# Two openings and the step between convolution and scan of a one-core vision kernel, put in another order

## What is computed

```
h = fno(x)                              # fc0, 4 x (rfft2, mix 20x20 modes, irfft2, pointwise, gelu), fc1, fc2
h = concat(cls_tok, h)                  # 128 x 65 tokens of 64 channels
h = h + attn(layernorm(h));  h = h + ffn(layernorm(h))

# inside attn, over windows of 32 tokens:
xm, z = split(x @ inproj_w.T);  xm = silu(causal_conv(xm, conv_w) + conv_b)
dt, B, C = split(xm @ xproj_w.T, [16, 32])            # 16, 16 and 16 columns
delta = softplus(dt @ dtproj_w.T + dtproj_b);  A = -exp(A_log)
h_t = exp(delta_t * A) * h_(t-1) + (delta_t * xm_t) * B_t
y_t = sum_n(h_t * C_t);  y = (y + xm * Dp) * silu(z);  out = y @ outproj_w.T
```

## Time and profile before

| | us |
|---|---|
| three runs | 6218.33, 6227.20, 6225.49 |
| their median | 6225.49 |
| the profiled execution, its own time | 6217.95 |
| its span | 6215.1 |
| first product of PE in the first program | 60.42 |
| last clearing barrier between the programs, first memset of POOL | 4846.69 |
| first turn of maps in the second program | 4894.87 |
| second block: first `draw` product, and its first sum of softplus | 5237.11, 5257.57 |

### The profile page before, as it was taken

One profiled execution on the slowest core, in us unless ns is written; L12 is line 12 of the kernel. 1 busy time (PEld: TensorE's weight loads), 2 busy tenths in 40 slices (PEclk: granted clock), 3 DMA queues, 4 the chain that ended last, 5 costly groups with the idle time before them and its releaser, 6 DMA issues. The chain is left out here.

```text
span 6215.1 us, 273887 instructions
## 1 busy us (share of the span) xinstructions
PE 5483.1 (88%) x119165; PEld 4105.8 (66%) x119165; DVE 2829.8 (46%) x4392; ACT 2677.2 (43%) x4990; POOL 1103.7 (18%) x1049
## 2 busy tenths in 40 slices
PE   5999999999999989989989999999999588888888
PEld 4877787677868876778677767876786243434343
DVE  2444344344434443444344434443443374848483
ACT  2334433443353335333533353344334364647473
POOL 3221222032203221222222122212220000000000
PEclk9999999999999999999999999999999798989898
DMA  2111111111111110111011101111110100000000
GB/s 33 15 14 15 20 14 14 15 19 14 14 17 18 14 22 12 15 21 18 10 20 19 14 14 21 14 15 17 14 14 4 22 1 8 1 8 1 4 1 4
DMA packets 443120, 85.55 MB, mean 14 GB/s; under 512 B 437624, under 2 KB 437896, under 8 KB 441832
## 3 DMA queue, kind: packets, MB, share of 16 engines
q1 hardware_dynamic: 441960, 67.78, 8.7%
HBM read 63.52 MB, written 4.23 MB: 11 GB/s over the span
## 5 line engine op out<-in xcount | busy, mean ns | idle before, releaser
L217 POOL COPY x_T<-x_X 128x512 f32<-128x512 f32 x1024 | 1074.5, 1105 | 3586.0 <-ACTq L791 3418.4
L786 ACT ACTIVATE x_X<-ga 128x512 f32<-128x512 f32 x1280 | 751.8, 598 | 1083.3 <-PE ga L458 899.2
L642 DVE COPY x_X<-ev 128x512 f32<-128x512 f32 x640 | 438.7, 689 | 842.5 <-PE ev L477 793.0
L458 PEld LDWEIGHTS ga<-pw_rhs,x_X 64*64 64x64 f32 x32768 | 595.0, 135 | 279.5 <-issue 278.2
L642 DVE COPY V<-ev 104x512 f32<-104x512 f32 x608 | 411.5, 690 | 599.3 <-PE ev L424 440.4
L489 PEld LDWEIGHTS ev<-dft_consts,x_T 128*64 128x64 f32 x16384 | 577.1, 137 | 42.0 <-issue 41.8
L489 PE MATMUL ev<-dft_consts,x_T 128*64 128x80 f32 x16384 | 598.1, 233 | 4.9 <-POOL x_T L217 3.4
L458 PE MATMUL ga<-pw_rhs,x_X 64*64 64x64 f32 x32768 | 587.0, 218 | 4.8 <-issue 4.1
L450 PE MATMUL ga<-V,inv_w 40*64 40x512 f32 x4096 | 550.0, 604 | 28.9 <-ACT V L754 27.9
L642 DVE COPY Y<-ev 128x400 f32<-128x400 f32 (+1 forms) x768 | 463.3, 603 | 208.5 <-PE ev L489 164.4
L642 DVE COPY D<-ev 128x512 f32<-128x512 f32 x576 | 362.3, 685 | 337.8 <-PE ev L396 335.5
(11 more groups left out here) (213 smaller groups left out, 8216.4 us busy)
## 6 DMA issues: line engine op xcount, KB each, us to landing
mix_w<-in_sw SPq DMA_DIRECT2D x128, 400.0 KB, 8.0
coords<-in_coords SPq DMA_DIRECT2D x66, 96.0 KB, 2.1
maps<-Y SPq DMA_DIRECT2D x128, 16.0 KB
raw<-maps SPq DMA_DIRECT2D x8, 256.0 KB, 3.6
out<-out_t SPq DMA_DIRECT2D x8, 256.0 KB, 3.5
w<-in_w SPq DMA_DIRECT2D x3, 512.0 KB, 6.6
fc_rhs<-in_fc_w SPq DMA_DIRECT2D x32, 0.4 KB
dft_consts<-in_dft SPq DMA_DIRECT2D x1, 336.0 KB
```

Source lines behind the costliest of these rows:

```text
L217: pool.tensor_copy(x_T[:, :, H * bc + h0:H * bc + h0 + 16].rearrange("p c (s n) -> p c s n", n=2), blocks.rearrange("p (s a n c) -> p a c ...
L458: last = pe.matmul(ps[HALF * bp:HALF * bp + HALF, HALF * s:HALF * s + HALF], x_X[r:r + HALF, g, col:col + HALF], pw_rhs[r:r + HALF, :], st ...
L642: dve.tensor_copy(dst, src).then_inc(ev_taken, 1)
L786: x_new = act.activation(blocks.rearrange("p (s a n) -> p s a n", s=8, a=2)[:, :, bc, :], ga[n % N_GA][:, :].rearrange("p (s n) -> p s n", ...
```

## The change

In `fno_program` the opening is ordered by need. POOL sets `fc0_rhs` and `coords` first, then S and `mix_w`; DVE clears the other six tiles itself. SP issues group 0's coordinates, the lower half of `fc0_rhs`, group 1's coordinates, and then the other small loads, which PE now waits for only ahead of the first mixing. ACT issues the Fourier constants, the bias columns and the upper half of `fc0_rhs` on its own queue (22 DMAs). The unused coordinates at the end are loaded ahead of the last maps' stores.

In `token_program` POOL clears the padded tiles first; ACT issues 18 `early` DMAs, SP the raw maps of block 0 and then the rest. `sel` and the bf16 identity are made by POOL, with no memset of `sel`. PE waits for the `later` weights only ahead of the product with `inproj`, and no longer for A (though it still waits for `out_ready`, which DVE signals behind A's sign change).

Between convolution and scan, B and C are made by one product of 32 columns, and `xc` is gone. DVE copies B, and splits C on token rows (128 partitions, 256 columns, into `gate_p`, which the experts use later); eight bf16 products turn the parts to where the spread reads them, and DVE copies them to `parts`. ACT loads the Exp table behind Silu by a one-column Exp, takes abs and exp by pieces, and ln by pieces; DVE adds by pieces as they come.

```
+        zeroed_pool = [S[:, :, :, :, :].rearrange("p a g b k -> p (a g b k)"),
+                       mix_w[:, :, :].rearrange("p a b -> p (a b)")]
+        zeroed_dve = [inv_h[:, :], pw_all[:, :, :].rearrange("p a b -> p (a b)"),
+                      fc2_lhs[:, :, :].rearrange("p a b -> p (a b)"), dc_bias[:, :, :].rearrange("p a b -> p (a b)"),
+                      D[:, :, :].rearrange("p a b -> p (a b)"), V[:, :, :].rearrange("p a b -> p (a b)")]
...
+            pool.memset(fc0_rhs[:, :], 0.0).then_inc(cleared, 1)
+            pool.memset(coords[:, :, :].rearrange("p a n -> p (a n)"), 1.0).then_inc(cleared, 1)
+            for tile in zeroed_pool:
                 pool.memset(tile, 0.0).then_inc(cleared, 1)
...
+        first_act = [(consts[:, :], t["dft"])]
+        for l in range(LAYERS):
+            first_act.append((cb_raw[:, l:l + 1], t["cb"][l].rearrange("(c a) -> c a", a=1)))
+        first_sp, once = [], []
+        for r, queue in ((0, first_sp), (HALF, first_act)):
+            for h in range(16):
+                queue.append((fc0_rhs[r + 3 * h:r + 3 * h + 3, CH * h:CH * h + CH], t["fc0_w"]))
+            queue.append((fc0_rhs[r + 48:r + 49, :].rearrange("p (h c) -> p h c", c=CH),
+                          t["fc0_b"].rearrange("(a x c) -> a x c", a=1, x=1).to_broadcast([1, 16, CH])))
+        N_FIRST = 16 * (len(first_sp) + len(first_act))
...
+            sp.wait_ge(cleared, 2)
             load_coords(0, 0)
-            load_coords(0, 1)
             with nc.allow_non_contiguous_dma(reason="small weights, once"):
+                for dst, src in first_sp:
+                    sp.dma_start(dst, src).then_inc(first_in, 16)
+                load_coords(0, 1)
+                sp.wait_ge(dve_cleared, len(zeroed_dve))
                 for dst, src in once:
-                    sp.dma_start(dst, src).then_inc(const_in, 16)
+                    sp.dma_start(dst, src).then_inc(mixw_in, 16)
+            sp.wait_ge(cleared, 2 + len(zeroed_pool))
             load_mix(0)
...
+                if last_coords is not None:
+                    last_coords()
...
+            pe.wait_ge(first_in, N_FIRST)
...
+                    pe.wait_ge(mixw_in, (chunk * LAYERS + to + 1) * (16 * J) + 16 * len(once))
...
+            pe.wait_ge(bias_ready, 1)
...
+            for tile in zeroed_dve:
+                last = dve.memset(tile, 0.0)
+                last.then_inc(dve_cleared, 1)
+            dve.wait_ge(dve_cleared, len(zeroed_dve))
+            dve.wait_ge(first_in, N_FIRST)
...
+            dve.wait_ge(cleared, 2 + len(zeroed_pool))
...
+            act.wait_ge(cleared, 2)
+            with nc.allow_non_contiguous_dma(reason="small weights, once"):
+                for dst, src in first_act:
+                    act.dma_start(dst, src).then_inc(first_in, 16)
...
-        xc = sb("xc", [DI, 2, 2 * DS])
-        padded.append(xc[:, :, :].rearrange("p h n -> p (h n)"))
-        for hf in range(2):
-            loads.append((xc[:, hf, DS * hf:DS * hf + DS], t["xproj"][:, DTR + DS:DTR + 2 * DS]))
...
+        first_tiles = {id(tile) for tile in (ident, center, average, cls, in_w, in_b, ln_g, ln_b, xproj, dtproj, A)}
+        early = [(tile, src) for tile, src, of in loads if id(of) in first_tiles]
+        later = [(tile, src) for tile, src, of in loads if id(of) not in first_tiles]
+        N_ZERO = 1 + len(decay)
...
+            for tile in padded:
+                pool.memset(tile, 0.0).then_inc(S_(padded_ready), 1)
             pool.memset(eps[:, :], EPS).then_inc(S_(zeroed), 1)
...
+            pool.wait_ge(S_(early_in), 16 * len(early))
+            pool.wait_ge(S_(zeroed), N_ZERO)
+            pool.tensor_copy(ident16[:, :], ident[:, :]).then_inc(S_(ident16_ready), 1)
+            pool.wait_ge(S_(ident16_ready), 1)
+            for q in range(3):
+                if q:
+                    pool.wait_ge(S_(sel_ready), q)
+                r = slice(32 * q, 32 * q + 32)
+                pool.tensor_copy(sel[r, :, :], ident[r, r].rearrange("p (n a) -> p n a", a=1).to_broadcast([32, 32, P]))\
+                    .then_inc(S_(sel_ready), 1)
...
-            sp.wait_ge(S_(zeroed), N_ZERO)
-            with nc.allow_non_contiguous_dma(reason="small weights, once"):
-                for dst, src in loads:
-                    sp.dma_start(dst[tuple(slice(None) for _ in dst.shape)], src).then_inc(S_(weights_in), 16)
-                sp.dma_start(gate_b[:, :], t["gate_b"].rearrange("(a e) -> a e", a=1).to_broadcast([P, NE]))\
-                    .then_inc(S_(weights_in), 16)
...
             load_raw(0)
+            sp.wait_ge(S_(padded_ready), len(padded))
+            with nc.allow_non_contiguous_dma(reason="small weights, once"):
+                for dst, src in later:
+                    sp.dma_start(dst[tuple(slice(None) for _ in dst.shape)], src).then_inc(S_(weights_in), 16)
+                sp.dma_start(gate_b[:, :], t["gate_b"].rearrange("(a e) -> a e", a=1).to_broadcast([P, NE]))\
+                    .then_inc(S_(weights_in), 16)
...
+            pe.wait_ge(S_(early_in), 16 * len(early))
+            pe.transpose(psB[0:DTR, 0:DI], xproj[:, 0:DTR], ident[:, :]).then_inc(S_(xdt_turned), 1)
             pe.wait_ge(S_(xdt_ready), 1)
-            pe.matmul(psA[:, BC:BC + DI], xdt_t[:, :], dtproj[:, :], start=True, stop=True).then_inc(S_(draw_w_made), 1)
-            pe.wait_ge(S_(consts_ready), 1)
+            pe.matmul(psB[:, BC:BC + DI], xdt_t[:, :], dtproj[:, :], start=True, stop=True).then_inc(S_(draw_w_made), 1)
...
+                pe.wait_ge(S_(weights_in), 16 * (len(later) + 1))
...
-                    for hf in range(2):
-                        at = HB * hf + c
-                        last = pe.matmul(psB[0:2 * DS, c:c + n], xc[:, hf, :], u[:, at:at + n],
-                                         start=hf == 0, stop=hf == 1)
-                last.then_inc(S_(xbc_ready), 1)
+                wait(sz_ready)
                 for j, (c, n) in enumerate(rows):
-                    last = pe.matmul(psB[0:n, HB + DS * j:HB + DS * j + DS], u[:, c:c + n], xproj[:, DTR:DTR + DS],
-                                     start=True, stop=True)
-                if win == 1:
-                    for j, (c, n) in enumerate(rows):
-                        last = pe.matmul(psB[0:n, HB + BC + DS * j:HB + BC + DS * j + DS], u[:, c:c + n],
-                                         xproj[:, DTR + DS:DTR + 2 * DS], start=True, stop=True)
+                    last = pe.matmul(psB[0:n, HB + 2 * DS * j:HB + 2 * DS * j + 2 * DS], u[:, c:c + n],
+                                     xproj[:, DTR:DTR + 2 * DS], start=True, stop=True)
                 last.then_inc(S_(b_turned), 1)
-                wait(pos_ready, len(cuts))
                 if win > 1:
-                    wait(parts_ready)
+                    pe.wait_ge(S_(ident16_ready), 1)
+                    wait(c_split)
+                    for j in range(nt):
+                        last = pe.matmul(psB[0:96, P * j:P * j + P], gate_p[:, j, :, :].rearrange("p s a -> p (s a)"),
+                                         ident16[:, :], start=True, stop=True)
+                    last.then_inc(S_(cT_ready), 1)
...
+                    wait(parts_ready)
...
+                pe.wait_ge(S_(sel_ready), 3)
...
+            act.wait_ge(S_(padded_ready), len(padded))
+            with nc.allow_non_contiguous_dma(reason="small weights, once"):
+                for dst, src in early:
+                    act.dma_start(dst[tuple(slice(None) for _ in dst.shape)], src).then_inc(S_(early_in), 16)
+            act.wait_ge(S_(early_in), 16 * len(early))
...
+                act.activation(std_first[:, :], eps[:, :], ACT.Exp)
                 for c, n in cuts:
                     wait(draw_ready)
 
                     act.activation(both(delta, w, c, n), paired(psA, c, n), ACT.Abs, bias=dt_b[:, :])\
                         .then_inc(S_(abs_ready), 1)
-                wait(b_turned)
+                    wait(abs_ready)
+                    act.activation(both(delta, w, c, n), both(delta, w, c, n), ACT.Exp, scale=-1.0)\
+                        .then_inc(S_(exp_ready), 1)
+                for c, n in cuts:
+                    wait(exp_ready)
+                    act.activation(both(delta, w, c, n), both(delta, w, c, n), ACT.Ln, bias=1.0).then_inc(S_(ln_ready), 1)
                 m = 2 * NT if w == BLK else 2
-                act.activation(b_t[0:tp, 0:m, :], psB[0:tp, HB:HB + DS * m].rearrange("p (j n) -> p j n", n=DS), ACT.Copy)\
-                    .then_inc(S_(b_copied), 1)
-                wait(abs_ready, len(cuts))
...
-            dve.wait_ge(S_(weights_in), 16 * (len(loads) + 1))
             dve.wait_ge(S_(zeroed), N_ZERO)
-            for q in range(3):
-                r = slice(32 * q, 32 * q + 32)
-                dve.tensor_copy(sel[r, :, :], ident[r, r].rearrange("p (n a) -> p n a", a=1).to_broadcast([32, 32, P]))
-            dve.tensor_copy(ident16[:, :], ident[:, :])
```

(33 more changed lines are left out.)

84 lines of the change are left out of this document (24 added, 60 removed).

## The result

| | before | after |
|---|---|---|
| runs, us | 6217.9 to 6227.2 (4 runs) | 6132.2 to 6140.61 (4 runs) |
| median, us | 6221.91 | 6139.37 |
| profiled execution, its span | 6217.95, 6215.1 | 6138.44, 6135.5 |

The ratio of the times is 0.9867, with a 95% interval of 0.9848 to 0.9887: faster by 1.3%. The forecast was 6132.8 with a range of 6110 to 6156. The time lies 6.6 us above the forecast and inside the range. Between the two profiled executions 79.6 us of span went, where my sum had 92.7. The table follows the same events through both traces; a row's gain is what is added to the lead on the way to that event.

What follows compares the result with a forecast made beforehand. Bound mostly by the untouched Fourier network (some 4775 of 6215 us); touched were idle openings and block chains. 45.7 + 4.0 + 32.6 - 11 + 19.2 + 2.2 = 92.7, from 6225.5 to 6132.8; range 6110 to 6156.

Steps and rivals of the forecast that it cites:

- rival (3): Both openings: two issue queues are no faster than one; time 6146, chance 0.08.
- PE waits 2 us: First opening: PE wants group 2's coordinates at 40.1, they land behind `mix_w` at 42, so it waits 2 us.
- the middle of two theories: Second opening: POOL's casts cost DVE between 0 and 22 us; the forecast took 11.
- rival (1): Second opening: POOL's casts hold DVE in full, 17 to 22 instead of 11; time 6139 to 6144, chance 0.20.
- 3c less 4.6: Second opening: three DVE operations wait c - 1.2, c - 2.4 and c - 1.0 for a cast of c.
- With the rise in the middle of them: Between convolution and scan: PE's clock rises during second `draw` or B and C; gain 4 to 5 a block, 4.8 taken.
- it never rises, gain 2: Between convolution and scan: PE's clock stays low, B and C end at 5253.3, gain 2 us a block.
- upper clock, 6.9: Between convolution and scan: PE at its upper clock, the sum starts at 5250.6, gain 6.9 us a block.
- (2): Second opening: POOL's casts cost DVE nothing; time 6122, chance 0.12.
- (4): Between convolution and scan: PE's clock is up in all four blocks, gain 28 instead of 19; time 6124, chance 0.08.
- (5): Scan: PE stays at its lower clock, a step costs up to 3.2 more; slower than before, 6261 with 40 steps, chance 0.03.
- (6): First opening: loads still end with the `once` list, 18 us of the gain go; time 6151, chance 0.04.

Runs made afterwards that it cites:

- the casts held back: The change with POOL's three casts of `sel` held back until block 0's input projection is there: 0.9858 of before, `inproj` 33.8 us behind the barrier (change 44.0).
- this part alone: The kernel before with only the change between convolution and scan: 0.9951 of before.
- the product in halves: The change with the product of B and C in halves, the first half's 16 matmuls between the two draws: 0.9867 of before.

## Why the prediction was right, and where its steps were not

- **First opening, 45.7 forecast, 39.8 measured at the projection of group 3.** The start was right: 13.42 instead of 12.7, ACT's list from 2.19 to 10.76 (forecast 2.3 to 10.3), and two queues as fast as hoped, so rival (3) fell. The failed step is "PE waits 2 us". The wait was named and its place was right, its size was not: `mix_w` took 10.75 us to issue, not 8.4, the coordinates were issued at 39.10, not at 36.9, and landed 6 us later. And the sum left out the clock: a wait of 4.1 us cost 7.2 to 7.4 with the lower clock behind it. The last 6.3 us up to the network's end are inside the scatter between executions, which no sum could have had.
- **End of the first program, 4.0 forecast, 5.1 measured.** The fc2 product is followed by the barrier within 6.8 us instead of 11.8. Right, a little small.
- **Second opening, 32.6 forecast, 32.3 measured.** The turn of the maps stands 15.9 behind the barrier (15.7 to 16). The early weights landed about 0.9 us later than forecast. What made that up is that A's sign change was not in the way: `out_ready` went out at 4824.0, when that operation began and not when it was over, so the step "PE still waits behind DVE's two copies, A's sign change and `out_ready`, 2.5 in all" was too long by 0.6: it took 1.9.
- **POOL's casts, 11 forecast, 9.6 measured, 10.2 against the casts held back.** The number was right by luck, as it was the middle of two theories. The mechanism was that of rival (1), with c = 3.63 instead of 7 to 8.8: the three operations took 7.9 us longer than usual (2.12 + 3.15 + 3.09 less 3 x 0.17), of which 5.75 reached PE. The prediction's own formula, 3c less 4.6, gives 6.3 with this c (and 16.4, not 17, at c = 7). The other 3.8 us are a term that neither theory had: PE, idle behind the operations, ran the variance and spread products at the lower clock. The mis-sized term is the cast. It was costed at the rate of POOL's copy of 512 columns, and went 2.4 times as fast. The rule of the Trainium skill, SBUF — State Buffer, section "Who interferes with whom", that the second of the two waits for the whole instruction of the other, agrees with the ends of the three operations, which fall on the ends of the casts within 0.03 us. As a mechanism it was better than the middle; with the cast priced at 8.8 it would have given 22, further off than the 11.
- **Between convolution and scan, 19.2 forecast, 13.3 measured** (22.0 in the trace of this part alone). The pieces are as forecast: second `draw` at +5.3, 3.78 or 2.0 long, ACT ready at 13.7 (forecast 13.5), the product 3.65 to 4.1 or 6.87 (3.75 or 7.3). Two steps failed. "With the rise in the middle of them" assumed that PE's clock would rise during the second `draw` or the product, as it had in the kernel before; it stays down through a product of 6.87 us in about half of the blocks, and in the product in halves it stays at 0.50 for the last 10.2 of 12.7 busy us. So the case "it never rises, gain 2" (2.0 to 2.7 measured) and the case "upper clock, 6.9" (5.9) both occur, about evenly. And I did not see that DVE waits in the wrong order, though the price of the product stood in the text: putting the sums first makes the stretch 17.1 to 17.5 at either clock.
- **Tail, 2.2 forecast, 2.3 measured.** The first sum starts 3.7 us behind `draw` instead of 6.2, and DVE's idle time in front of it fell from 2.78 to 1.09 us.
- **Other rivals.** (2) fell with the 9.6 us, (4) with three of four blocks at the lower clock, (5) since from `draw` to the gate turn a block at the lower clock takes 187.4 us and at the upper one 184.1, and 3.1 of these 3.3 are the step itself (21.5 and 18.35), so there is no slower scan behind it; from the turns of `du` on, a block took no longer than before. (6) fell with the first product at 13.42.
- **The sum.** 92.7 less 5.2 (stall) less 6.3 (network) less 5.9 (blocks), plus 2.7 elsewhere in the blocks and 1.6 in the small terms, is 79.6. By medians the gain is 82.5 us (6221.91 to 6139.37), 10.2 less than the sum. The time itself was missed by only 6.6, since the median of before came down from 6225.5 to 6221.9 with its fourth run: that part is luck.

## What to carry to other kernels

Order each engine's list by when its inputs come, not by what belongs together: a copy that waits for a slow product holds whatever stands behind it on its engine. Work that was given to POOL "beside" DVE held DVE's small operations between SBUF tiles, and did not hold its convolution, which reads PSUM: put such work there, or cut it into small instructions. Where loads are brought forward, follow the queue past the part that was moved: the next stall is behind the next big transfer, and PE's clock nearly doubled its price here (4.1 us of waiting, 7.4 in all).
